# A factorization tower on one core: the last tile's softmax in two parts, its field jobs partly inside the loop

## The chip, the core and the metric

The kernel runs on one core of one Trainium2 chip. The metric is the device time of one execution in microseconds, less is better; a run of the kernel before took 1276.11 us in the median of three (1275.78 to 1276.74).

## The reference, cut to what matters

For each of 1024 samples, 33 rows of 128 numbers are gathered from 33 tables. All 528 pairs of them are multiplied element by element, go through a linear layer with relu, and are scored against a feature row of the sample. A softmax over the 528 scores weights the pair products, whose sum goes into a small perceptron.

```
inner = x[:, row] * x[:, col]                      # [1024, 528, 128]
fm = relu(einsum('bpd,ad->bpa', inner, attn_W) + attn_b)
scores = einsum('ba,bpa->bp', gnn_feature, fm)
attn = softmax(scores, axis=1)
attn_output = einsum('bp,bpd->bd', attn, inner) * 100.0
h = relu(concat([gnn_feature, attn_output, gnn_feature]) @ W_top1 + b_top1)
y = relu(h @ W_top2 + b_top2) @ W_top3
```

## The kernel before

The samples go in T = 8 tiles of 128, and a tile in STEPS = 32 steps of GROUPS = 4 samples; S counts the ALL = 256 steps of the program, s those within a tile t. The code is one block per engine, with semaphores between them, and the order of the work is written out by hand.

In step S, DVE multiplies the pairs of step S + 3 (`product`, L405) and forms the low part of step S + 1 (`rest_of_inner`, L412); ACT rounds the high part of S + 2 (`round_inner`, L298) and takes the hidden layer out of PSUM with bias and relu (`relu`, L290); PE runs `hidden(S)` (L534 for a native chunk, L541 to L543 for three passes of a split one). Per step 5 chunks, one of them native, two in the steps with s in NATIVE_2 = (2, 5, 8, 11, 14, 17); the remainder that ACT and DVE treat is then 1688 or 1696 columns, or 1264 or 1272. Behind every second step `reduce_steps` (L564) adds two steps' rows to `scores`: matmuls with a block matrix that put the scores of sample 32 j + s into row 32 j + s and add zeros elsewhere. PSUM has three banks for hidden chunks and all other jobs, in a ring in the order of `units`; `claim` waits until the bank's last user was taken out.

The softmax of tile t - 1 runs in the first steps of tile t: row maximum on DVE (L426, s = 1), exponentials on ACT (L305, s = 2), reciprocal of the sum on DVE (L430, s = 2), scaling on ACT into `attn` (L313, s = 3), and `turn_attn` on DVE (s = 4): the far half of the pairs is added (L436) and the matrix is transposed in blocks of 32 into `attn_turned` (L439). PE may begin the next tile's scores only behind the exponentials. SP then copies `attn_turned` in four pieces of partitions per job into the zero-filled `attn_t` (`spread_attn`, L207) and loads the rows of the fields from DRAM (`load_fields`, L202). Four `fields` jobs follow on PE (L592, at s = 7, 10, 13, 16), each for 32 samples, that is 8 steps; DVE multiplies each by x (`weigh`, L447) and sums it (`sum_weighted`, L454). Three `mlp` jobs end the tile.

The last tile has no next one. Behind step 255 come, in order: the softmax, ACT and DVE copying attn_turned into attn_t and into a part of `inner` that POOL has zeroed (L382, L386, L508, L512), all four jobs, with the fields of jobs 2 and 3 from `x_rows`, four products and sums, and the perceptron. PE fills pauses with `keep_clock` (L621): matmuls whose result nobody reads, 12, 8, 3 and 3 of them.

## Time and profile before

| | |
|---|---|
| median of 3 runs | 1276.11 us |
| the profiled execution: time | 1276.58 us |
| the profiled execution: span | 1274.3 us |
| PE busy | 1207.8 us, 95% |
| DVE busy | 1150.6 us, 90% |
| ACT busy | 1018.7 us, 80% |
| POOL busy | 465.7 us, 37% |

The span runs from the first to the last instruction of the profiled execution; its own time is 2.3 us longer. A row of a timeline gives the start in us from the span's start, the duration, the engine, the line, the operation, its tiles as out<-in, the shape, the number of merged instructions (x2) and, in brackets, the idle time before it and what ended it. PE's records of an fp32 matmul are two per instruction.

### The profile page before, as it was taken

How to read it: one execution, taken by the hardware profiler on the slowest of the kernel's cores; microseconds unless marked ns; L12 is line 12 of the kernel's file. 1: busy time of each engine (PE TensorE's matmuls, PEld its weight loads, DVE VectorE, ACT ScalarE, POOL GpSimd, SP SyncE). 2: the span in 40 equal slices, each digit the busy share in tenths (PEclk: the TensorE clock that was granted, in tenths of full speed). 3: DMA queues.
4: the chain of work that ended last, by engine and by line, in shares of the span. 5: the costliest groups of instructions: out<-in, count | busy, mean ns of one | idle time of the engine just before them, and what ended most of it. 6: DMA issues, size and time to landing. Idle time of an engine off the chain costs nothing.

```text
span 1274.3 us, 21264 instructions
## 1 busy us (share of the span) xinstructions
PE 1207.8 (95%) x8752; PEld 902.5 (71%) x8752; DVE 1150.6 (90%) x643; ACT 1018.7 (80%) x1038; POOL 465.7 (37%) x271
## 2 busy tenths in 40 slices
PE   1499999999999999999999999999999999999998
PEld 1277777777777777777767777677776777777776
DVE  2399899998999989998999989999899998999974
ACT  1288998778887888878897788877888788887882
POOL 6586684018810387006840088102880000000000
PEclk9999999999999999999999999999999999999999
DMA  4213211311103111131102211031111300012100
GB/s 107 101 34 96 55 30 28 110 36 30 30 18 126 30 27 32 30 106 36 32 21 58 93 30 32 18 110 41 30 32 31 107 17 1 1 30 57 31 1 1
DMA packets 54287, 58.47 MB, mean 46 GB/s; under 512 B 10536, under 2 KB 48560, under 8 KB 53168
## 3 DMA queue, kind: packets, MB, share of 16 engines
q1 hardware_dynamic: 45728, 39.81, 10.5%
q0 software_dynamic: 8448, 17.32, 5.2%
q8 instruction: 69, 1.13, 0.4%
q14 instruction: 26, 0.21, 0.1%
q10 hardware_dynamic: 16, 0.00, 0.0%
HBM read 36.12 MB, written 17.31 MB: 42 GB/s over the span
## 4 chain that ended last, share of the span: by engine, by line
PE 78%; ACT 7%; issue 7%; DVE 6%; POOL 2%; DMA 0%; DVEq 0%; ACTq 0%; POOLq 0%
PE scores L564 18%; PE ring L534 16%; PE ring L541 12%; PE ring L542 11%; PE ring L543 11%; PE ring L592 3%; ACT fm L290 3%; DVE inner L405 3%; POOL x_rows L259 2%; PE ring L574 2%; ACT inner_hi L298 2%; DVE inner_lo L412 2%; PE ring L610 1%; DVE attn L447 1%; PE scores L621 1%
## 5 line engine op out<-in xcount | busy, mean ns | idle before, releaser
L290 ACT ACTIVATE fm<-ring,attn_b_sb 128x848 f32<-128x848 f32 (+1 forms) x640 | 596.9, 971 | 182.1 <-PE ring L534 175.7
L405 DVE TENSOR_TENSOR inner<-xt 128x2112 f32<-128x2112 f32 x256 | 602.7, 2354 | 67.5 <-ACT xt L328 37.4
L259 POOL DMA_INDIRECT x_rows<-in_tbl,ids_all x264 | 463.2, 1754 | 490.9 <-PE ring L574 401.2
L412 DVE TENSOR_TENSOR inner_lo<-inner,inner_hi 128x1688 fp32r<-128x1688 f32 (+4 forms) x256 | 467.0, 1824 | 25.8 <-ACT inner_hi L298 22.8
L541 PE MATMUL ring<-inner_hi,attn_wt_lo 128*128 128x424 f32 (+1 forms) x971 | 434.8, 448 | 4.2 <-ACT fm L290 3.5
L298 ACT CAST inner_hi<-inner 128x1688 fp32r<-128x1688 f32 (+4 forms) x256 | 392.3, 1532 | 5.1 <-DVE inner L405 5.0
L542 PE MATMUL ring<-inner_lo,attn_wt_hi 128*128 128x424 f32 (+1 forms) x971 | 344.3, 355 | 0.0
L543 PE MATMUL ring<-inner_hi,attn_wt_hi 128*128 128x424 f32 (+1 forms) x971 | 344.1, 354 | 0.0
L534 PE MATMUL ring<-inner,attn_wt 128*128 128x424 f32 (+1 forms) x618 | 276.6, 544 | 10.2 <-issue 6.5
L564 PE MATMUL scores<-fm,gnn_blocks 128*32 128x264 f32 x4096 | 254.6, 389 | 5.5 <-ACT exp_pairs L305 5.5
L541 PEld LDWEIGHTS ring<-inner_hi,attn_wt_lo 128*128 128x128 f32 x971 | 182.8, 188 | 71.8 <-issue 39.1
L542 PEld LDWEIGHTS ring<-inner_lo,attn_wt_hi 128*128 128x128 f32 x971 | 183.3, 189 | 43.5 <-issue 40.3
L564 PEld LDWEIGHTS scores<-fm,gnn_blocks 128*32 128x32 f32 x4096 | 119.9, 109 | 107.2 <-issue 13.9
L543 PEld LDWEIGHTS ring<-inner_hi,attn_wt_hi 128*128 128x128 f32 x971 | 182.5, 188 | 5.5
L534 PEld LDWEIGHTS ring<-inner,attn_wt 128*128 128x128 f32 x618 | 104.8, 190 | 85.5 <-issue 76.9
L274 POOL MEMSET inner<- 128x2048 f32 x1 | 1.8, 1811 | 279.0 <-PE ring L543 279.0
L574 PE MATMUL ring<-ident,x_rows 128*128 128x128 f32 x264 | 39.2, 292 | 34.1 <-DMA x_rows<-in_tbl,ids_all 31.3
L328 ACT COPY xt<-ring 128x1024 f32<-128x1024 f32 (+1 forms) x40 | 38.5, 966 | 31.6 <-PE ring L574 20.8
L574 PEld LDWEIGHTS ring<-ident,x_rows 128*128 128x128 f32 x264 | 33.0, 151 | 39.6 <-DMA x_rows<-in_tbl,ids_all 25.2
L592 PE MATMUL ring<-attn_t,x_fields 128*128 128x128 f32 x480 | 58.3, 275 | 1.1 <-issue 1.1
L592 PEld LDWEIGHTS ring<-attn_t,x_fields 128*128 128x128 f32 x480 | 58.0, 191 | 1.7 <-issue 1.5
L447 DVE TENSOR_TENSOR attn<-ring,xt 128x1024 f32<-128x1024 f32 x32 | 39.0, 1219 | 3.2 <-PE ring L592 2.9
(50 smaller groups left out, 250.3 us busy)
## 6 DMA issues: line engine op xcount, KB each, us to landing
x_dram<-x_rows SPq DMA_DIRECT2D x8, 2112.0 KB, 6.6
x_fields<-x_dram SPq DMA_DIRECT2D x120, 128.0 KB, 3.0
x_rows<-in_tbl,ids_all POOLq DMA_INDIRECT x264
attn_t<-attn_turned SPq DMA_DIRECT2D x112, 32.0 KB, 1.9
w_sb<-in_W_top SPq DMA_DIRECT2D x2, 512.0 KB
x_rows<-x_dram SPq DMA_DIRECT2D x8, 128.0 KB, 3.9
x_fields<-in_r_gnn_feature SPq DMA_DIRECT2D x1, 512.0 KB
h<-in_W_top SPq DMA_DIRECT2D x1, 256.0 KB
```

What stands on the lines that cost most here:

```text
L259: nc.gpsimd.indirect_dma_start(out=x_rows[:, f, :], out_offset=None, in_=tables[f], in_offset=bass.IndirectOffsetOnAxis(ap=ids_all[:, t, f ...
L290: nc.scalar.activation(dst, slot(("hidden", pair, j))[:, :, 0:n], ACT.Relu, bias=attn_b_sb[:, 0:1]).then_inc(s_fm, 1)
L298: nc.scalar.copy(inner_hi[:, S % HI_BUFS, 0:COLS - at], inner[:, S % INNER_BUFS, at:]).then_inc(s_hi, 1)
L405: nc.vector.tensor_tensor(dst, a, b, ALU.mult).then_inc(s_inner, 1)
L412: nc.vector.tensor_tensor(inner_lo[:, S % LO_BUFS, 0:COLS - at], inner[:, S % INNER_BUFS, at:], inner_hi[:, S % HI_BUFS, 0:COLS - at].bitc ...
L534: nc.tensor.matmul(dst, attn_wt[:], inner[:, S % INNER_BUFS, begin:end], start=True, stop=True)\
L541: nc.tensor.matmul(dst, attn_wt_lo[:], hi, start=True, stop=False)
L542: nc.tensor.matmul(dst, attn_wt_hi[:], lo, start=False, stop=False)
L543: nc.tensor.matmul(dst, attn_wt_hi[:], hi, start=False, stop=True).then_inc(s_hidden, 1)
L564: last = nc.tensor.matmul(scores[I * j:I * j + I, h, 0:HALF], block_of(s, j), fm[:, S % FM_BUFS, at:at + HALF], start=s == 0, stop=s == ST ...
L574: last = nc.tensor.transpose(to[:, n // 4, n % 4 * P:(n % 4 + 1) * P], x_rows[:, FU * c + n, :], ident[:])
L592: last = nc.tensor.matmul(bank[:, h, to:to + QS * I], x[:, n, :], own[:, :, n, :], start=True, stop=True)
```

## The change

The table PART_END has nine parts in place of eight tiles: seven tiles, then 248 and 256. Part 7 is the first 24 steps (96 samples) of the last tile, and its softmax runs at steps 249 to 252. The scores stay in place and the last 8 steps are added; part 8 then repeats the softmax over all rows. Jobs 0 and 1 of the last tile stand behind `hidden(253)` and `hidden(254)`, with copies by SP; job 2 stands behind the last scores, from the same part 7. Only job 3 needs part 8. For it ACT scales the first 16 rows of the matrix and DVE the other 16, DVE transposes these first, then adds the far part and transposes the rest; the copies into attn_t are of 256 elements in place of twice 512. Job 3's products and sums go in halves of 16 samples, with job 2's sum between them. POOL's memset and the loads into x_rows are gone, and of the fillers 6 and 4 remain of 12 and 8.

```diff
+
+    PART_END = [STEPS * (t + 1) for t in range(T - 1)] + [ALL - FN, ALL]
+
+    def part_at(S, after):
+
+        return PART_END.index(S - after) if S - after in PART_END else None
+
+    LAST_FIELDS_AT = (ALL - 3, ALL - 2)
+
...
+        if S in LAST_FIELDS_AT:
+            jobs.append(("fields", T - 1, LAST_FIELDS_AT.index(S)))
         return jobs
...
-    units += [("fields", T - 1, c) for c in range(FJ)] + [("mlp", T - 1, n) for n in range(3)]
+    units += [("fields", T - 1, c) for c in (2, 3)] + [("mlp", T - 1, n) for n in range(3)]
...
-        TAIL_INNER = (ALL - 3) % INNER_BUFS
-        attn_t_tail = inner[:, TAIL_INNER, 0:2 * QS * FN * I].rearrange("p (c q n i) -> p c q n i", c=2, q=QS, n=FN)
-        x_fields_tail = x_rows[:, 0:2 * FN, :].rearrange("p (c n) d -> p c n d", c=2)
+        weighted_tail = inner[:, 0, 0:QS * FN * I].rearrange("p (b f) -> p b f", f=I)
...
-            sp.wait_ge(s_store, 16 * T)
-            sp.wait_ge(s_xt_done, XJ * T)
-            load_fields(T - 1, 2, x_fields_tail[:, 0], s_fields_tail)
-            load_fields(T - 1, 3, x_fields_tail[:, 1], s_fields_tail)
+            sp.wait_ge(s_inv, 3 * T)
+            spread_attn(0)
+            spread_attn(1)
+            sp.wait_ge(s_fields_done, FJ * (T - 1) + 1)
+            load_fields(T - 1, 2, x_fields[:, 0], s_fields[0])
+            spread_attn(2)
+            sp.wait_ge(s_fields_done, FJ * (T - 1) + 2)
+            load_fields(T - 1, 3, x_fields[:, 1], s_fields[1])
...
-            pool.wait_ge(s_lo, ALL - 2)
-            pool.wait_ge(s_hidden, CHUNKS * (ALL - 2))
-            nc.gpsimd.memset(inner[:, TAIL_INNER, 0:2 * QS * FN * I], 0.0).then_inc(s_tail_zero, 1)
...
+            def scale_attn(p):
+                act.wait_ge(s_inv, 3 * p + 1)
+                if p > 0:
+                    act.wait_ge(s_pooled, FJ * p if p < T else FJ * T - 2)
+                rows = I if p < T else K
+                src = exp_pairs[:].rearrange("b (i c) -> b i c", c=FX)[:, 0:rows, 1:F]
+                nc.scalar.activation(attn[:, 0:rows, :], src, ACT.Copy, scale=inv_sum[:, 0:1]).then_inc(s_attn, 1)
...
-                if s == EXP_AT and t > 0:
-                    exps(t - 1)
+                if part_at(S, EXP_AT) is not None:
+                    exps(part_at(S, EXP_AT))
                 if S + 2 < ALL:
                     round_inner(S + 2)
-                if s == SCALE_AT and t > 0:
-                    scale_attn(t - 1)
+                if part_at(S, SCALE_AT) is not None:
+                    scale_attn(part_at(S, SCALE_AT))
...
-            exps(T - 1)
-            scale_attn(T - 1)
-            act.wait_ge(s_inv, 3 * T)
-            act.wait_ge(s_fields_done, FJ * (T - 1))
-            act.wait_ge(s_tail_zero, 1)
+            exps(T)
+            scale_attn(T)
+            act.wait_ge(s_tail_high, 2)
+            act.wait_ge(s_inv, 3 * (T + 1))
+            act.wait_ge(s_fields_done, FJ * T - 2)
             for q in range(QS // 2):
                 own = slice(q * I, (q + 1) * I)
-                nc.scalar.copy(attn_t[own, :, q], attn_turned[own, 0:2 * FN, :].rearrange("p (c n) i -> p c n i", c=2))\
-                    .then_inc(s_tail_attn, 1)
-            for q in range(QS // 2):
-                own = slice(q * I, (q + 1) * I)
-                nc.scalar.copy(attn_t_tail[own, :, q], attn_turned[own, 2 * FN:, :].rearrange("p (c n) i -> p c n i", c=2))\
-                    .then_inc(s_tail_attn, 1)
+                nc.scalar.copy(attn_t[own, (FJ - 1) % 2, q], attn_turned[own, (FJ - 1) * FN:, :]).then_inc(s_tail_attn, 1)
...
+            def row_max(p):
+                dve.wait_ge(s_red, PART_END[p] // 2)
...
+            def add_far(p):
+                dve.wait_ge(s_attn, p + 1)
...
-                dve.wait_ge(s_inv, 3 * t + 2)
+                dve.wait_ge(s_inv, 3 * p + 2)
+
+            def turn_attn(p):
+                add_far(p)
                 nc.vector.transpose(attn_turned[:].rearrange("p n i -> p i n"), attn[:]).then_inc(s_inv, 1)
+
+            def turn_last_attn():
+                turned = attn_turned[:].rearrange("p n i -> p i n")
+                src = exp_pairs[:].rearrange("b (i c) -> b i c", c=FX)[:, K:I, 1:F]
+                dve.wait_ge(s_inv, 3 * T + 1)
+                nc.vector.tensor_scalar(attn[:, K:I, :], src, inv_sum[:, 0:1], None, ALU.mult).then_inc(s_tail_high, 1)
+                dve.wait_ge(s_tail_high, 1)
+                dve.wait_ge(s_spread[0], 16 * QS * (FJ // 2 * (T - 1) + 2))
+                nc.vector.transpose(turned[:, K:I, :], attn[:, K:I, :]).then_inc(s_tail_high, 1)
+                add_far(T)
+                nc.vector.transpose(turned[:, 0:K, :], attn[:, 0:K, :]).then_inc(s_inv, 1)
...
-                nc.vector.tensor_tensor(weighted, y, xt[:, t % 2, own, 0:I], ALU.mult).then_inc(s_weighted, 1)
+                dst = weighted if (t, c) != (T - 1, 2) else weighted_tail
+                nc.vector.tensor_tensor(dst, y, xt[:, t % 2, own, 0:I], ALU.mult).then_inc(s_weighted, 1)
...
+            def last_weighted_sum():
+                first, half = P - QS * FN, QS * FN // 2
+                y = slot(("fields", T - 1, FJ - 1))
+                for h in range(2):
+                    own = slice(first + h * half, first + (h + 1) * half)
+                    part = weighted[:, h * half:(h + 1) * half, :]
+                    if h == 0:
+                        dve.wait_ge(s_half, 1)
+                    else:
+                        dve.wait_ge(s_fields_done, FJ * T)
+                    nc.vector.tensor_tensor(part, y[:, h, :].rearrange("d (b f) -> d b f", f=I), xt[:, (T - 1) % 2, own, 0:I],
+                                            ALU.mult).then_inc(s_half_weighted if h == 0 else s_weighted, 1)
+                    if h == 0:
+                        dve.wait_ge(s_half_weighted, 1)
+                    else:
+                        dve.wait_ge(s_weighted, FJ * T)
+                    nc.vector.tensor_reduce(pooled[:, own], part, AX.X, ALU.add)\
+                        .then_inc(s_half_pooled if h == 0 else s_pooled, 1)
+                    if h == 0:
+                        sum_weighted(T - 1, 2)
+                dve.wait_ge(s_half_pooled, 1)
+                dve.wait_ge(s_pooled, FJ * T)
+                nc.vector.tensor_scalar(pooled[:], pooled[:], 100.0, None, ALU.mult).then_inc(s_pooled100, 1)
...
-                if s == TURN_AT and t > 0:
-                    turn_attn(t - 1)
+                if part_at(S, TURN_AT) is not None:
+                    turn_attn(part_at(S, TURN_AT))
...
+                if part_at(S, MAX_AT) is not None:
+                    row_max(part_at(S, MAX_AT))
                 if s == MAX_AT and t > 0:
-                    row_max(t - 1)
                     gnn_block(t)
-                if s == INV_AT and t > 0:
-                    invert_sum(t - 1)
-            row_max(T - 1)
-            invert_sum(T - 1)
-            turn_attn(T - 1)
-            dve.wait_ge(s_inv, 3 * T)
-            dve.wait_ge(s_fields_done, FJ * (T - 1))
-            dve.wait_ge(s_tail_zero, 1)
+                if part_at(S, INV_AT) is not None:
+                    invert_sum(part_at(S, INV_AT))
+            row_max(T)
+            invert_sum(T)
+            turn_last_attn()
+            dve.wait_ge(s_inv, 3 * (T + 1))
+            dve.wait_ge(s_tail_high, 2)
+            dve.wait_ge(s_fields_done, FJ * T - 2)
             for q in range(QS // 2, QS):
...
+                nc.vector.tensor_copy(attn_t[own, (FJ - 1) % 2, q], attn_turned[own, (FJ - 1) * FN:, :]).then_inc(s_tail_attn, 1)
+            weigh(T - 1, 2)
+            last_weighted_sum()
...
+                if S0 in PART_END:
+                    pe.wait_ge(s_exp, PART_END.index(S0) + 1)
                 if s0 == 0:
-                    if t > 0:
-                        pe.wait_ge(s_exp, t)
                     pe.wait_ge(s_blocks, t + 1)
...
-                if t < T - 1:
+                pe.wait_ge(s_fields[c % 2], 16 * QS * (FJ // 2 * t + c // 2 + 1))
+                if (t, c) != (T - 1, FJ - 1):
                     pe.wait_ge(s_spread[c % 2], 16 * QS * (FJ // 2 * t + c // 2 + 1))
-                    pe.wait_ge(s_fields[c % 2], 16 * QS * (FJ // 2 * t + c // 2 + 1))
-                elif c < 2:
-                    pe.wait_ge(s_tail_attn, 2 * QS)
-                    pe.wait_ge(s_fields[c], 16 * QS * (FJ // 2 * t + 1))
                 else:
-                    own, x = attn_t_tail[:, c % 2], x_fields_tail[:, c % 2]
-                    pe.wait_ge(s_fields_tail, 2 * 16 * QS)
+                    pe.wait_ge(s_tail_attn, QS)
                 for n in range(FN):
                     h, to = divmod(n * QS * I, 512)
                     last = nc.tensor.matmul(bank[:, h, to:to + QS * I], x[:, n, :], own[:, :, n, :], start=True, stop=True)
+                    if (t, c) == (T - 1, FJ - 1) and n == FN // 2 - 1:
+                        last.then_inc(s_half, 1)
...
-            pe.wait_ge(s_exp, T)
-            keep_clock(12)
-            for c in range(FJ):
-                fields(T - 1, c)
-            keep_clock(8)
+            fields(T - 1, 2)
+            pe.wait_ge(s_exp, T + 1)
+            keep_clock(6)
+            fields(T - 1, 3)
+            keep_clock(4)
```

DVE's last steps, before: from the remainder of step 250 on (inner_lo is the remainder, inner the product).

```order
L412 TENSOR_TENSOR inner_lo<-inner,inner_hi 128x1688
L405 TENSOR_TENSOR inner<-xt 128x2112
L412 TENSOR_TENSOR inner_lo<-inner,inner_hi 128x1696
L405 TENSOR_TENSOR inner<-xt 128x2112
L412 TENSOR_TENSOR inner_lo<-inner,inner_hi 128x1688
L405 TENSOR_TENSOR inner<-xt 128x2112
L412 TENSOR_TENSOR inner_lo<-inner,inner_hi 128x1696
L405 TENSOR_TENSOR inner<-xt 128x2112
L412 TENSOR_TENSOR inner_lo<-inner,inner_hi 128x1688
L412 TENSOR_TENSOR inner_lo<-inner,inner_hi 128x1696
```

And now, from the product of step 252 on:

```order
L413 TENSOR_TENSOR inner<-xt 128x2112
L434 TENSOR_REDUCE neg_max<-scores 128x1
L420 TENSOR_TENSOR inner_lo<-inner,inner_hi 128x1696
L413 TENSOR_TENSOR inner<-xt 128x2112
L438 RECIPROCAL inv_sum<-exp_sum 128x1
L420 TENSOR_TENSOR inner_lo<-inner,inner_hi 128x1688
L413 TENSOR_TENSOR inner<-xt 128x2112
L420 TENSOR_TENSOR inner_lo<-inner,inner_hi 128x1696
L444 SCALAR_TENSOR_TENSOR attn<-exp_pairs,inv_sum,attn 128x16x16
L450 STREAM_TRANSPOSE attn_turned<-attn 128x32x32
L413 TENSOR_TENSOR inner<-xt 128x2112
L420 TENSOR_TENSOR inner_lo<-inner,inner_hi 128x1688
```

Maximum, reciprocal, far part (L444) and transposition (L450) stand between the products and remainders of steps 251 to 255.

PE behind the last scores, before:

```order
L564 MATMUL scores<-fm,gnn_blocks 32x264 x16
L621 MATMUL scores<-fm,attn_wt 128x264 x12
L592 MATMUL ring<-attn_t,x_fields 128x128 x16
L592 MATMUL ring<-inner,x_rows 128x128 x16
L621 MATMUL scores<-fm,attn_wt 128x264 x8
L600 MATMUL ring<-gnn_t,w_sb 128x128 x4
L604 MATMUL ring<-pooled,w_sb 128x128 x4
```

And now:

```order
L607 MATMUL scores<-fm,gnn_blocks 32x264 x16
L631 MATMUL ring<-attn_t,x_fields 128x128 x8
L662 MATMUL scores<-fm,attn_wt 128x264 x6
L631 MATMUL ring<-attn_t,x_fields 128x128 x8
L662 MATMUL scores<-fm,attn_wt 128x264 x4
L641 MATMUL ring<-gnn_t,w_sb 128x128 x4
L645 MATMUL ring<-pooled,w_sb 128x128 x4
L662 MATMUL scores<-fm,attn_wt 128x264 x3
```

One job stands ahead of the first filler and one behind it. The two others stand in the loop; the first of them behind the last three-pass chunk of step 253 and ahead of the native chunk of step 254:

```order
L584 MATMUL ring<-inner_hi,attn_wt_lo 128x424
L585 MATMUL ring<-inner_lo,attn_wt_hi 128x424
L586 MATMUL ring<-inner_hi,attn_wt_hi 128x424
L631 MATMUL ring<-attn_t,x_fields 128x128 x8
L577 MATMUL ring<-inner,attn_wt 128x424
L584 MATMUL ring<-inner_hi,attn_wt_lo 128x424
```

## Rows read from the trace of the kernel before

**Rows 1.** The page, part 1: busy us (share of the span) of each engine, and instructions.

```profile
PE 1207.8 (95%) x8752; PEld 902.5 (71%) x8752; DVE 1150.6 (90%) x643; ACT 1018.7 (80%) x1038; POOL 465.7 (37%) x271
```

**Rows 2.** Timeline of PE behind the loop: start us, us, engine, line, op, tiles, count.

```profile
1246.76 5.61 PE L621 MATMUL scores<-fm,attn_wt 128*128 128x264 f32 x24 [2.09 <-ACT exp_pairs L305]
1253.49 3.81 PE L592 MATMUL ring<-attn_t,x_fields 128*128 128x128 f32 x32 [1.12 <-issue]
```

**Rows 3.** Timeline of DVE behind the loop.

```profile
1244.74 0.71 DVE L426 TENSOR_REDUCE neg_max<-scores 128x1 f32<-128x528 f32 x1 [8.33 <-PE scores L564]
1246.74 0.16 DVE L430 RECIPROCAL inv_sum<-exp_sum 128x1 f32<-128x1 f32 x1 [1.30 <-ACT exp_pairs L305]
1248.15 0.67 DVE L436 SCALAR_TENSOR_TENSOR attn<-exp_pairs,inv_sum,attn 128x256 f32<-128x256 f32 x1 [1.24 <-ACT attn L313]
1248.85 1.96 DVE L439 STREAM_TRANSPOSE attn_turned<-attn 128x1024 f32<-128x1024 f32 x1
1250.85 0.87 DVE L508 COPY attn_t<-attn_turned 32x512 f32<-32x512 f32 x2
...
1255.55 1.22 DVE L447 TENSOR_TENSOR attn<-ring,xt 128x1024 f32<-128x1024 f32 x1 [2.92 <-PE ring L592]
1256.81 1.22 DVE L454 TENSOR_REDUCE pooled<-attn 128x32 f32<-128x1024 f32 x1
...
1265.81 0.23 DVE L457 TENSOR_SCALAR pooled<-pooled 128x128 f32<-128x128 f32 x1
```

**Rows 4.** Timeline of ACT behind the loop.

```profile
1246.94 1.18 ACT L313 ACTIVATE attn<-exp_pairs,inv_sum 128x1024 f32<-128x1024 f32 x1 [0.23 <-DVE inv_sum L430]
1250.85 1.26 ACT L382 COPY attn_t<-attn_turned 32x512 f32<-32x512 f32 x2 [2.73 <-DVE attn_turned L439]
```

**Rows 5.** Timeline of PE, steps 224 to 232: matmuls of one pair of steps onto scores.

```profile
1099.62 1.99 PE L564 MATMUL scores<-fm,gnn_blocks 128*32 128x264 f32 x32
...
1108.75 1.99 PE L564 MATMUL scores<-fm,gnn_blocks 128*32 128x264 f32 x32 [0.77 <-ACT exp_pairs L305]
...
1117.69 1.99 PE L564 MATMUL scores<-fm,gnn_blocks 128*32 128x264 f32 x32
...
1125.97 1.99 PE L564 MATMUL scores<-fm,gnn_blocks 128*32 128x264 f32 x32
```

**Rows 6.** The same, steps 230 and 231.

```profile
1136.29 1.99 PE L564 MATMUL scores<-fm,gnn_blocks 128*32 128x264 f32 x32
```

**Rows 7.** The same, steps 248 to 251.

```profile
1220.86 1.99 PE L564 MATMUL scores<-fm,gnn_blocks 128*32 128x264 f32 x32
...
1229.08 1.99 PE L564 MATMUL scores<-fm,gnn_blocks 128*32 128x264 f32 x32
```

**Rows 8.** Timeline of DVE, step 228: the turn of tile 6.

```profile
1116.39 2.11 DVE L439 STREAM_TRANSPOSE attn_turned<-attn 128x1024 f32<-128x1024 f32 x1
```

**Rows 9.** The page, part 5: busy, mean ns of one | idle before, releaser.

```profile
L405 DVE TENSOR_TENSOR inner<-xt 128x2112 f32<-128x2112 f32 x256 | 602.7, 2354 | 67.5 <-ACT xt L328 37.4
...
L412 DVE TENSOR_TENSOR inner_lo<-inner,inner_hi 128x1688 fp32r<-128x1688 f32 (+4 forms) x256 | 467.0, 1824 | 25.8 <-ACT inner_hi L298 22.8
```

**Rows 10.** Timeline of ACT, steps 227 and 229: rounding of 1272 and 1696 columns.

```profile
1112.53 1.25 ACT L298 CAST inner_hi<-inner 128x1272 fp32r<-128x1272 f32 x1
...
1121.46 1.60 ACT L298 CAST inner_hi<-inner 128x1696 fp32r<-128x1696 f32 x1
```

**Rows 11.** Timeline of PE, step 228: a wait for ACT.

```profile
1115.77 0.46 PE L541 MATMUL ring<-inner_hi,attn_wt_lo 128*128 128x424 f32 x1 [0.51 <-ACT fm L290]
```

**Rows 12.** Timeline of the SP queue, step 228: the eight copies of attn_turned.

```profile
1118.53 4.94 SPq L207 DMA_DIRECT2D attn_t<-attn_turned  x8
```

**Rows 13.** DMA by tile, attn_t: time from issue to landing over all 112.

```profile
DMA to landing us min/median/max: 1.8/1.9/3.6
```

**Rows 14.** Busy time by engine (PE, PEld, DVE, ACT, POOL), PEclk, DMA share, GB/s.

```profile
1266.10:1274.30 8.20, 6.36 (x40) 5.04 (x40) 0.00 (x0) 2.02 (x7) 0.00 (x0) 1.00 0.00 1
```

**Rows 15.** Timeline of PE, first step of the program.

```profile
54.64 5.99 PE L534 MATMUL ring<-inner,attn_wt 128*128 128x424 f32 x8 [6.46 <-issue]
```

More of the change, by code:

```diff
@@ L306, in exps @@
                                      bias=neg_max[:, 0:1], accum_out=exp_sum[:, 0:1]).then_inc(s_exp, 1)
-            def scale_attn(t):
-                act.wait_ge(s_inv, 3 * t + 1)
-                if t > 0:
-                    act.wait_ge(s_pooled, FJ * t)
-                src = exp_pairs[:].rearrange("b (i c) -> b i c", c=FX)[:, 0:I, 1:F]
-                nc.scalar.activation(attn[:], src, ACT.Copy, scale=inv_sum[:, 0:1]).then_inc(s_attn, 1)
+            def scale_attn(p):
[5 more added lines that the diff above has]
+                nc.scalar.activation(attn[:, 0:rows, :], src, ACT.Copy, scale=inv_sum[:, 0:1]).then_inc(s_attn, 1)
             def repeat(t, c):
@@ L453, in sum_weighted @@
                     dve.wait_ge(s_mlp_done, 3 * (t - 1) + 1)
-                nc.vector.tensor_reduce(pooled[:, own], weighted, AX.X, ALU.add).then_inc(s_pooled, 1)
+                src = weighted if (t, c) != (T - 1, 2) else weighted_tail
+                nc.vector.tensor_reduce(pooled[:, own], src, AX.X, ALU.add).then_inc(s_pooled, 1)
                 if c == FJ - 1:
@@ L645, in _ @@
             reduce_steps(ALL - 2, True)
-            pe.wait_ge(s_exp, T)
-            keep_clock(12)
-            for c in range(FJ):
-                fields(T - 1, c)
-            keep_clock(8)
+            fields(T - 1, 2)
[3 more added lines that the diff above has]
+            keep_clock(4)
             for n in range(3):
```

27 lines of the change are left out of this document (8 added, 19 removed).

## The prediction

> **What bounds the kernel now.** First read the page's busy shares: PE is busy for 95% of the span and DVE for 90% [rows 1], so inside the loop an added matmul is paid in full, and added DVE or ACT work only as far as PE comes to wait for it. Then read the timelines behind the loop. There the order is another: from 1244.74, when DVE begins the last maximum, the work is one chain through the softmax, the turn, the copies into attn_t, four products and four sums on DVE, and the scaling of pooled, which ends at 1265.81 + 0.23 = 1266.04 [rows 3]. That chain is 21.30 us. The perceptron and the store behind it take another 8.2 us, 6.36 of them PE's [rows 14]. PE works in the 21.30 us too, but half of it is filler (5.61 us [rows 2]). So the change trades the time of a nearly idle tail against the time of a full loop, and the question is the rate of exchange. I call M the start of the last maximum, and count the tail from it.
>
> **Part 1: the second softmax inside the loop.** Part 7 (96 samples) runs its maximum, exponentials, scaling and turn at steps 249 to 252, placed as at a tile's border. The trace has this event seven times, so I price it from the last one, at steps 225 to 228. Between two plain pairs of score matmuls lie 1229.08 - 1220.86 = 8.22 us [rows 7]. At the border the same distances are 1108.75 - 1099.62 = 9.13, 1117.69 - 1108.75 = 8.94 and 1125.97 - 1117.69 = 8.28 [rows 5]: 0.91 + 0.72 + 0.06 over plain. The first surplus is PE's wait for the exponentials (0.77). The second holds a wait of 0.51 for a relu of ACT [rows 11], which ACT reaches late behind the scaling of attn. The third pair has a step with two native chunks, which the new place hasn't, so I drop the 0.06. Sum: 1.63 us. The new place is a little worse. At step 227 ACT rounds only 1272 columns (1.25 us), at step 251 it rounds a full remainder (1.60 us) [rows 10], ahead of the scaling and of the relu that PE waits for. I add the whole 0.35: **+1.98 us**. Ends: 1.63 (the ACT queue absorbs it) and 2.6 (the surplus is paid again in the next pair).
>
> **Part 2: jobs 0 and 1 of the last tile in the loop.** Two jobs behind the loop took 3.81 us [rows 2], so 1.90 each; inside the loop a pair with one job lasts 1136.29 - 1125.97 = 10.32 against 8.28, so 2.04 [rows 5, 6]. Nothing hides them, PE has no idle time there. I take 2 x 1.90 = **+3.80 us**, ends 3.6 and 4.1.
>
> **Part 3: do their operands come in time?** In the other tiles three steps lie between the turn and job 0, here one. At step 228 the transposition ends at 1116.39 + 2.11 = 1118.50 [rows 8]. SP issues the eight copies from 1118.53 in 4.94 us, 0.62 each, and one lands 1.9 us after its issue in the median [rows 12, 13]. Job 0 needs four: the fourth is issued at 1118.53 + 3 x 0.62 = 1120.4 and lands at 1122.3. PE would want it one score group and one step behind 1117.69: a plain pair is two steps and 1.99 of scores, so 1117.69 + 1.99 + (8.22 - 1.99) / 2 = 1122.8. Margin 0.5 us, and the later relu shifts PE by 0.35 more, while DVE's turn is some 0.2 later (a full remainder in place of a short one, no gnn blocks). So I cost it at nothing, and its upper end is 1.2: a landing of 3.6 us, the longest seen, less the 1.9 and the margin. Job 1 needs the eighth, issued at 1118.53 + 7 x 0.62 = 1122.9 and landed at 1124.8, and PE asks for them two us of job and three of matmuls later. Job 2's loads and copies (8 issues) start when job 0 is done, some 12 us ahead of the loop's end; job 3's loads start when job 1 is done. Both lie under steps 254 and 255.
>
> **Part 4: DVE's extra work in the loop.** Maximum, reciprocal, far half and transposition are 0.71 + 0.16 + 0.67 + 1.96 = 3.5 us [rows 3], and two products and sums follow. The cover is DVE's lead. Behind the transposition it owes one product (2.35) and the remainder for step 254 (1.9 at most [rows 9]: a full one is slower than the mean of 1.82), so it is done near 1118.5 + 4.3 = 1122.8 by the clock of step 228. PE needs that remainder behind job 0 and the first chunk of step 254, near 1125. From there DVE has no products left, only PE has. Cost nothing. Without that cover PE would wait the overshoot, and I keep 0.5 as the end. The POOL memset, the eight loads into x_rows and the filler go at no gain: nothing waited for them.
>
> Loop: 1.98 + 3.80 = **+5.8 us**, between 5.2 and 7.5.
>
> **Part 5: the new tail.** Maximum, exponentials and reciprocal are as before, ending at M + 2.16 (1246.74 + 0.16 [rows 3]). Job 2 on PE hides in the 2.09 us in which PE only waited for the exponentials [rows 2]. Then, on DVE:
> - scaling the upper 16 rows, 512 elements. No row shows it; a copy of 512 is 0.42 (0.87 for two), a reduction of 528 is 0.71 [rows 3]. It reads and writes SBUF as the copy does: 0.42, done M + 2.62. ACT scales the lower rows beside it, half of 1.18 and half its fixed share, 0.7 [rows 4], done M + 2.9, covered.
> - transposing half: 1.96 / 2 plus a few hundredths, 1.02; far part 0.67; the other half 1.02, with 0.03 between: M + 5.42. Before: 1250.81, M + 6.07.
> - copies of 256 elements, two on ACT and two on DVE. ACT took 1.26 for two of 512 [rows 4], 0.62 each. Its roundings give 0.35 us for 424 elements [rows 10], 0.83 ns per element, so 256 elements less are 0.21 less: 0.43 with gaps each, M + 6.31. Before there were four of 512 and PE began at 1253.49, M + 8.75; now M + 6.41.
> - DVE's own copies end near M + 6.02, then the product of job 2, 1.22, to M + 7.29. Half of job 3 is ready at M + 6.41 + 1.1 = 7.51 (a whole one took 1255.55 - 1253.49 = 2.06). Product of a half 0.71 (as the 528 of the maximum), sum of it 0.71, sum of job 2 1.22, product and sum of the second half 0.71 + 0.71, scaling 0.23, and 0.24 of gaps: 7.52 + 4.29 + 0.24 = M + 12.05.
>
> Before M + 21.30, now M + 12.05: **-9.3 us**. Ends: -9.8 (halves at exactly half) and -8.5 (the scaling 0.71, each half transposition 1.2, copies still 0.6). PE's part from there to the store is the same.
>
> A rule bears on the halves. By the row the ACT copy of 512 is 0.617, and the slope leaves 0.20 of it fixed. The Trainium skill, page "VectorE: DVE Perf Modes", section "The TRN2 errata — SBUF-src ops pay a fixed extra latency per instruction", says that splitting pays a fixed latency per piece, and gives ScalarE 224 cycles plus the elements. By its figures (an estimate) a copy of 256 is 0.40 us where I have 0.43, and the tail would be 0.06 shorter; for 512 the trace agrees, 0.61 to 0.62.
>
> **Sum.** +5.8 - 9.3 = -3.5 us. The profiled execution took 1276.58 (span 1274.3), 0.5 over the median of 1276.11. Against the median I forecast **1272.6 us**. A change within 0.2%, 2.55 us, is no change for a measurement of this kernel.
>
> **Rivals.**
> - *The turn comes too close to job 0.* The fourth copy lands late (1.2), or DVE's lead is short (0.5), or the border costs 2.6; the loop then pays 6.8 to 7.5 and 1.8 to 2.5 us are left: near 1274.0. For it: a margin of 0.5 us against a landing that varies by 1.8 [rows 13], and full remainders where the border has short ones. Against it: PE is delayed by the same ACT work. Chance 0.17.
> - *The clock falls in the tail (slower).* Twenty filler matmuls ahead of the perceptron become ten, and PE idles from M + 4.9 to M + 6.4. The granted clock is 1.00 (2.4 GHz) in the tail now [rows 14], behind idle stretches of 2.09 and 1.12 us [rows 2]. At the start, behind 6.46 us of idle, eight matmul records of 424 columns took 5.99 us, 0.75 each [rows 15]; the filler has 0.23 for 264 columns [rows 2], which is 0.38 for 424, so those ran at half pace. If the granted clock fell to 1.2 GHz at the last gap, 1.1 us of job 3 and the 6.36 us of PE behind the sum would double: +7.5 - 3.5 = +4.0, 1280.1 us. It decides if the clock is already down when job 3 begins. Against it: no new gap is longer than 2.09 us. The Trainium skill, page "TensorE: Matmul & The Clock Gate", section "What's actually happening", has throttled as the default state and activity as what releases it, which speaks against less filler; by it the time would be those 1280.1 us. Chance 0.05.
> - *The tail gains more.* Halves cost half, the ACT delay is absorbed: 5.3 - 9.8 = -4.5, 1271.6 us. Chance 0.10.
>
> **The numbers.** The forecast has 0.66, the rest 0.02. The range takes the ends of loop and tail, 1271.4 to 1274.7; outside are the clock and a border dearer than all seven seen. Faster by over 0.2% means below 1273.56: forecast, the better tail and a little of the first rival, 0.78. Same: most of that rival, 0.16. Slower: 0.06.
>
> **What would show it.** Last score matmul some 5.8 us later than at 1244.7; distances of about 9.1, 9.3 and 12.0 between the score groups of 246 to 252; PE waiting under 0.3 us ahead of job 0; from the maximum to the scaled pooled 12.0 us; PEclk 1.00 to the end. Wrong would be a wait for DMA ahead of job 0, a wait of PE for inner_lo at step 254, or matmul records of 0.75 us behind job 3.

## The result, and the profile after

| | before | changed |
|---|---|---|
| median | 1276.11 us (8 runs, 1275.73 to 1276.74) | 1272.16 us (8 runs, 1272.02 to 1272.48) |
| profiled execution, time | 1276.58 us | 1272.05 us |
| span | 1274.3 us | 1269.9 us |

The ratio is 0.9968, with a 95% interval of 0.9959 to 0.9977: 3.95 us faster. On the page the busy times hardly moved. PE has 4.3 us and 20 records less, which are the ten fillers; DVE has 2.7 us more [rows 1].

```profile
PE 1203.5 (95%) x8732; PEld 898.6 (71%) x8732; DVE 1153.3 (91%) x649; ACT 1018.9 (80%) x1039; POOL 465.4 (37%) x270
```

The timeline of PE at steps 246 to 255, with the score groups and the two jobs that now stand in the loop (start, duration, engine, line, form, in brackets the wait before it):

```profile
1212.27 1.99 PE L607 MATMUL scores<-fm,gnn_blocks 128*32 128x264 f32 x32
...
1221.40 1.99 PE L607 MATMUL scores<-fm,gnn_blocks 128*32 128x264 f32 x32 [0.85 <-ACT exp_pairs L317]
...
1228.77 0.46 PE L584 MATMUL ring<-inner_hi,attn_wt_lo 128*128 128x424 f32 x1 [0.87 <-ACT fm L302]
...
1230.70 1.99 PE L607 MATMUL scores<-fm,gnn_blocks 128*32 128x264 f32 x32
...
1235.74 1.95 PE L631 MATMUL ring<-attn_t,x_fields 128*128 128x128 f32 x16
...
1240.55 1.95 PE L631 MATMUL ring<-attn_t,x_fields 128*128 128x128 f32 x16
1242.42 1.99 PE L607 MATMUL scores<-fm,gnn_blocks 128*32 128x264 f32 x32
...
1247.70 2.23 PE L607 MATMUL scores<-fm,gnn_blocks 128*32 128x264 f32 x32
```

The distances between the groups are 1221.40 - 1212.27 = 9.13, 9.30, 11.72 and 5.28 us. In the kernel before they are 8.22, three times (one of them in [rows 7]), and 5.14. From the group of step 246 to DVE's last maximum it is 1249.99 - 1212.27 = 37.72 us, before 32.10 (from 1212.64 to 1244.74 [rows 3]). The loop is **5.62 us longer**: 0.91 and 1.08 us at the new border, 3.50 in the distance that holds both jobs, and 0.14 in the last. The two waits of PE in it are those that the border of a tile has: 0.85 for the exponentials, 0.87 for a relu of ACT [rows 5, 11: 0.77 and 0.51]. Ahead of job 0 at 1235.74 PE waits for nothing.

The timeline of DVE behind the loop, which answers to [rows 3]:

```profile
1249.99 0.71 DVE L434 TENSOR_REDUCE neg_max<-scores 128x1 f32<-128x528 f32 x1 [4.98 <-PE scores L607]
...
1252.19 0.48 DVE L456 TENSOR_SCALAR attn<-exp_pairs,inv_sum 128x512 f32<-128x512 f32 x1
1252.71 1.08 DVE L459 STREAM_TRANSPOSE attn_turned<-attn 128x512 f32<-128x512 f32 x1
1253.65 0.58 DVE L444 SCALAR_TENSOR_TENSOR attn<-exp_pairs,inv_sum,attn 128x256 f32<-128x256 f32 x1
1254.26 1.05 DVE L461 STREAM_TRANSPOSE attn_turned<-attn 128x512 f32<-128x512 f32 x1
1255.35 0.61 DVE L557 COPY attn_t<-attn_turned 32x256 f32<-32x256 f32 x2
1255.99 1.23 DVE L470 TENSOR_TENSOR inner<-ring,xt 128x1024 f32<-128x1024 f32 x1
1257.54 0.69 DVE L493 TENSOR_TENSOR attn<-ring,xt 128x512 f32<-128x512 f32 x1 [0.33 <-PE ring L631]
1258.27 0.69 DVE L499 TENSOR_REDUCE pooled<-attn 128x16 f32<-128x512 f32 x1
1258.87 1.21 DVE L478 TENSOR_REDUCE pooled<-inner 128x32 f32<-128x1024 f32 x1
1259.99 0.68 DVE L493 TENSOR_TENSOR attn<-ring,xt 128x512 f32<-128x512 f32 x1
...
1261.50 0.23 DVE L505 TENSOR_SCALAR pooled<-pooled 128x128 f32<-128x128 f32 x1
```

From the start of the maximum to the end of the scaling of pooled it is 1261.73 - 1249.99 = **11.74 us, before 21.30**. The transposed matrix is complete at +5.32 (before +6.07), and two products and two sums of a whole job are gone.

ACT's scaling of half a matrix and its two copies [rows 4], and PE around them [rows 2]:

```profile
1252.19 0.74 ACT L326 ACTIVATE attn<-exp_pairs,inv_sum 128x512 f32<-128x512 f32 x1 [0.23 <-DVE inv_sum L438]
1255.39 0.83 ACT L395 COPY attn_t<-attn_turned 32x256 f32<-32x256 f32 x2 [2.46 <-DVE attn_turned L461]
```

```profile
1249.85 2.05 PE L631 MATMUL ring<-attn_t,x_fields 128*128 128x128 f32 x16
...
1256.37 2.02 PE L631 MATMUL ring<-attn_t,x_fields 128*128 128x128 f32 x16 [1.42 <-ACT attn_t L395]
```

Job 2 runs while DVE and ACT are at the maximum and the exponentials. Behind the scaled pooled both kernels take 8.22 us to the end of the span. So +5.62 - 9.56 = -3.94 us by the two traces, against -3.95 by the medians. The remaining 0.4 us between the two spans lies ahead of step 222, in code that the change doesn't touch: its scores start at 1099.62 before and at 1099.26 after.

### The profile page after: what moved, and what is told of

The parts are those of the page before. It is cut to its first block, busy times and chain, and to the rows that moved or that the text cites. A ratio compares the mean times of both kernels' runs of the same rounds, so it can differ in the third digit from the quotient of the medians.

```text
span 1269.9 us, 21243 instructions
## 1 busy us (share of the span) xinstructions
PE 1203.5 (95%) x8732; PEld 898.6 (71%) x8732; DVE 1153.3 (91%) x649; ACT 1018.9 (80%) x1039; POOL 465.4 (37%) x270
## 4 chain that ended last, share of the span: by engine, by line
PE 77%; ACT 8%; issue 7%; DVE 6%; POOL 2%; DMA 0%; DVEq 0%; ACTq 0%; POOLq 0%
PE scores L607 18%; PE ring L577 16%; PE ring L584 12%; PE ring L585 11%; PE ring L586 11%; ACT fm L302 3%; PE ring L631 3%; DVE inner L413 3%; ACT inner_hi L310 3%; POOL x_rows L274 2%; PE ring L617 2%; DVE inner_lo L420 2%; PE ring L651 1%; ACT exp_pairs L317 1%; DVE attn L470 1%
## 5 line engine op out<-in xcount | busy, mean ns | idle before, releaser
L631 PE MATMUL ring<-attn_t,x_fields 128*128 128x128 f32 x512 | 62.5, 275 | 1.4 <-ACT attn_t L395 1.4
L631 PEld LDWEIGHTS ring<-attn_t,x_fields 128*128 128x128 f32 x512 | 61.9, 191 | 2.4 <-issue 2.2
L478 DVE TENSOR_REDUCE pooled<-attn 128x32 f32<-128x1024 f32 x30 | 36.4, 1214 | 0.1
```

The lines of the kernel that those rows point to most:

```text
L631: last = nc.tensor.matmul(bank[:, h, to:to + QS * I], x[:, n, :], own[:, :, n, :], start=True, stop=True)
```

## The experiments

Runs 1 to 4 were made on chip 11 and runs 5 to 12 on chip 0, where the kernel before takes 1273.28 us (beside runs 1 to 4), 1273.94 (5 to 8) and 1273.18 (9 to 12). Most of the difference from 1276.11 lies ahead of the first scores (67.5 us into the span of the changed kernel above, 64.8 in run 12), so distances inside a trace are compared. All runs but 10 and 12 are single executions. For the changed kernel these are, above and within 0.01 us in run 12 too, 37.72 us from the scores of step 246 to the last maximum (the loop's end), 11.74 us from there to the scaled pooled (the tail), and 8.22 us to the end. The edits of runs 1, 2 and 4 don't touch the loop, and it takes 37.71 to 37.72 us in them; those of runs 5 to 8 don't touch the tail, and it takes 11.74 to 11.75. So a difference of 0.1 us between two such distances is clear of noise. M + x is x us behind the start of the last maximum.

**1. Job 3 in one piece.** Is the order of job 3's halves and job 2's sum worth something?

```diff
-            weigh(T - 1, 2)
-            last_weighted_sum()
+            for c in (2, 3):
+                weigh(T - 1, c)
+                sum_weighted(T - 1, c)
```

> Job 3's product and sum in one piece, behind job 2's sum; the turn stays in halves. Theory 1 (DVE bounds the last stage, and job 2 covers PE's part): job 3 is ready 8.4 us behind the start of the last maximum (6.4 + 2.0), and DVE reaches it at 8.5 anyway (copies done at 6.0, product 1.23, sum 1.21). So the halves start nothing earlier and only pay the fixed share of two more instructions: scaled pooled at 11.3 us in place of 11.74, the run 0.4 us shorter. Theory 2 (the halves let DVE begin half a job earlier): 12.3 to 12.5, 0.6 us longer.

Measured: loop 37.72, tail **11.32**, 0.42 less. DVE's timeline, with M at 1247.13:

```profile
1254.39 1.22 DVE L478 TENSOR_REDUCE pooled<-inner 128x32 f32<-128x1024 f32 x1
1255.71 1.23 DVE L470 TENSOR_TENSOR attn<-ring,xt 128x1024 f32<-128x1024 f32 x1
1256.97 1.22 DVE L478 TENSOR_REDUCE pooled<-attn 128x32 f32<-128x1024 f32 x1
1258.23 0.23 DVE L481 TENSOR_SCALAR pooled<-pooled 128x128 f32<-128x128 f32 x1
```

Job 3 is complete on PE at M + 8.41, and DVE takes it at M + 8.58, directly behind job 2's sum. Halves can't end the chain earlier, because job 2's product and sum fill the time. They cost the fixed share of two more instructions (twice 0.69 for the halves against 1.23 for a whole product, and much the same for the sum, 0.3 us in all). In the order of the changed kernel DVE also waits 0.33 us for the first half of job 3 (at 1257.54 above) while job 2's sum stands ready; run 1 has no such wait. The overlaps between instructions take a part of the two back. Theory 1 holds. This part of the change loses time.

**2. The turn in one piece.** ACT scales all 32 rows, one transposition; job 3 stays in halves.

```diff
-                rows = I if p < T else K
+                rows = I
...
-            turn_last_attn()
+            dve.wait_ge(s_spread[0], 16 * QS * (FJ // 2 * (T - 1) + 2))
+            turn_attn(T)
...
```

> Scaling on ACT of all 32 rows and one transposition, as before the change; job 3's products stay in halves. Theory 1 (the split puts DVE's scaling and first transposition beside ACT's scaling): the transposition ends 6.07 us behind the start of the maximum in place of 5.32, and all behind it moves by 0.75: the run 0.75 us longer. Theory 2 (the fixed share of the added instructions eats it): below 0.3 us longer.

Measured: tail 12.46, **0.72 more**. With M at 1246.96:

```profile
1250.44 0.66 DVE L443 SCALAR_TENSOR_TENSOR attn<-exp_pairs,inv_sum,attn 128x256 f32<-128x256 f32 x1 [1.31 <-ACT attn L326]
1251.13 1.92 DVE L449 STREAM_TRANSPOSE attn_turned<-attn 128x1024 f32<-128x1024 f32 x1
```

DVE waits 1.31 us for ACT's scaling, which the split fills with its own half, and the transposition ends at M + 6.09 in place of 5.32. Theory 1 holds: of the two things that the change does in halves, this one pays.

**3. Job 1 behind the scores.** Only job 0 stays in the loop, and job 1's product goes into another buffer.

```diff
-    LAST_FIELDS_AT = (ALL - 3, ALL - 2)
+    LAST_FIELDS_AT = (ALL - 3,)
...
+            fields(T - 1, 1)
             fields(T - 1, 2)
...
+            weigh(T - 1, 1)
+            sum_weighted(T - 1, 1)
             weigh(T - 1, 2)
             last_weighted_sum()
```

> Job 1 behind the scores too, so that only job 0 stands in the loop; DVE's product and sum of job 1 come ahead of those of job 2. Theory 1 (a job costs the loop 1.87 us of PE and spares the tail 2.5 us of DVE): loop 1.9 us shorter, tail 2.5 us longer, the run 0.6 us longer. Theory 2 (the tail has idle DVE time and takes the job for nothing): 1.9 us shorter.

Measured: loop 35.83 (-1.89), tail 13.94 (+2.20), and 9.43 us behind it in place of 8.22, which neither theory had. The perceptron's first product with pooled on PE, and two stretches of the windows view (the stretch and its length, busy us of PE, PEld, DVE, ACT and POOL, then PEclk, DMA share and GB/s):

```profile
1259.04 2.08 PE L648 MATMUL ring<-pooled,w_sb 128*128 128x128 f32 x8 [2.88 <-DVE pooled L506]
```

```profile
1256.00:1259.00 3.00, 0.16 (x2) 0.00 (x0) 2.85 (x5) 0.00 (x0) 0.00 (x0) 0.94 0.00 0
1259.00:1261.00 2.00, 1.96 (x9) 1.96 (x10) 0.00 (x0) 0.00 (x0) 0.00 (x0) 0.50 0.00 0
```

PE waited 2.88 us for the longer tail, the granted clock fell to half (1.2 GHz) before the wait was over, and eight records took 2.08 us in place of 1.16. So this run didn't price the job alone. Run 11 repeats it with nine fillers in place of four.

```diff
-            keep_clock(4)
+            keep_clock(9)
```

> Job 1 behind the scores as before, with nine filler matmuls in place of four ahead of the perceptron. Theory 1 (the perceptron ran slow there because the clock fell in a PE pause of 2.9 us, and the job's own balance is 1.93 us less in the loop and 2.2 more in the tail): granted clock 1.00 to the end, 8.2 us from the scaled pooled to the end in place of 9.43, and 0.3 us longer than the changed kernel from the first scores to the end. Theory 2 (something else slows the perceptron): 9.4 us stay.

```profile
1256.00:1260.00 4.00, 3.34 (x24) 2.96 (x23) 2.72 (x5) 0.00 (x0) 0.00 (x0) 1.00 0.00 0
1260.00:1267.10 7.10, 5.28 (x33) 3.96 (x31) 0.00 (x0) 2.02 (x7) 0.00 (x0) 1.00 0.00 0
```

Measured: clock 1.00, 8.21 us behind the tail, loop 35.81, tail 13.93: -1.91 + 2.19 = **+0.28 us** on the changed kernel. A job in the loop costs 1.9 us there and spares the tail 2.2. That is the rate of exchange, and it is thin: the times of single executions don't resolve it (1269.14 us here, 1269.12 to 1269.74 for the changed kernel in run 12).

**4. No filler.** The other question of the clock: do the ten fillers that are left hold it?

```diff
-            keep_clock(6)
             fields(T - 1, 3)
-            keep_clock(4)
```

> The ten filler matmuls ahead of the perceptron left out (they compute nothing that is read). PE then idles from 2.0 to 6.4 us behind the start of the maximum. Theory 1 (this idle time is short enough for the clock to stay at 2.4 GHz): granted clock 1.00 to the end, job 3 at 2.0 us, the run as long as the changed kernel within 0.2 us. Theory 2 (filler is what holds the clock): granted clock below 1 behind job 3 or in the perceptron, the records there of up to twice the length, and the run up to 7.5 us longer.

```profile
1253.20 3.26 PE L631 MATMUL ring<-attn_t,x_fields 128*128 128x128 f32 x16 [4.42 <-ACT attn_t L395]
```

```profile
1249.00:1253.00 4.00, 0.00 (x0) 0.00 (x0) 3.80 (x8) 1.49 (x3) 0.00 (x0) 1.00 0.00 0
1253.00:1254.30 1.30, 1.10 (x7) 1.13 (x8) 1.04 (x1) 0.05 (x1) 0.00 (x0) 0.78 0.01 6
1254.30:1256.50 2.20, 2.20 (x13) 2.20 (x12) 1.67 (x3) 0.00 (x0) 0.00 (x0) 0.50 0.00 0
```

Measured: through the 4.42 us of idle PE the granted clock is still 1.00. It falls when job 3 has begun (0.78 in the mean of 1253.0 to 1254.3, 0.50 behind it), job 3 takes 3.26 us in place of 2.02, and the tail 12.12, **0.38 more**. From 1258 on the clock is 1.00 again and the perceptron takes its usual 8.21. Theory 2 is right that the clock falls without the fillers, and the price is far below its upper end: DVE's work on job 2 covers most of a slow job 3 (DVE waits 0.75 us for its first half in place of 0.33), and the clock is back before the perceptron. The Trainium skill, page "TensorE: Matmul & The Clock Gate", section "What's actually happening", calls the throttled state the default that activity lifts; the traces agree in both runs: 0.50 behind pauses of 2.88 and 4.42 us, and 1.00 again while PE works.

**5. Jobs 0 and 1 one step earlier.** How near are the copies of attn_turned to job 0?

```diff
-    LAST_FIELDS_AT = (ALL - 3, ALL - 2)
+    LAST_FIELDS_AT = (ALL - 4, ALL - 3)
```

> Jobs 0 and 1 one step earlier, behind steps 252 and 253. Theory 1 (part 3 of the prediction: the fourth copy of attn_turned lands just ahead of job 0, 0.45 us in the changed kernel, and one place earlier PE would wait for it): PE asks for it at the place where the scores of step 250 began, 1230.7, the copy lands at 1235.3, a wait of 4.6 us, and the loop is 4 to 4.7 us longer. Theory 2 (there is slack behind the turn that the forecast did not count): below 1 us longer.

```profile
1232.54 3.75 PE L631 MATMUL ring<-attn_t,x_fields 128*128 128x128 f32 x16 [4.58 <-DMA attn_t<-attn_turned]
```

```profile
1235.00:1240.00 5.00, 5.00 (x42) 2.84 (x41) 2.44 (x2) 0.00 (x0) 0.00 (x0) 0.68 0.36 104
```

Measured: PE waits **4.58 us** for the DMA, as theory 1 has it. The loop is 45.18 us though, 7.46 more: in that pause the clock fell too. It is 0.50 from 1232 to 1238 (0.68 in the mean of 1235 to 1240), job 0 took 3.75 us, and what follows it is slow until the clock has risen. Six us at half the clock are 3 us lost, by estimate, and 7.46 - 4.58 = 2.88 were. No theory had that. In the changed kernel SP issues the eight copies here:

```profile
1231.63 4.94 SPq L218 DMA_DIRECT2D attn_t<-attn_turned  x8
```

The fourth is issued at 1231.63 + 3 x 0.62 = 1233.5 and lands 1.9 later [rows 13], at 1235.4; PE takes job 0 at 1235.74.

**6. The exponentials ahead of the relu.** Three relus stand on ACT between the maximum and the exponentials. This moves the exponentials up by one relu, at all eight borders inside the loop.

```diff
-                relu(S // 2, 2 if S % 2 else 0)
                 if part_at(S, EXP_AT) is not None:
                     exps(part_at(S, EXP_AT))
+                relu(S // 2, 2 if S % 2 else 0)
```

> On ACT the exponentials stand ahead of the first relu of their step in place of behind it, at all eight borders inside the loop. Theory 1 (PE's wait of 0.77 to 0.85 us at a border is ACT's queue: the maximum is there 1.9 us before the exponentials begin, and three relus stand between): first distance at a border 8.3 in place of 9.14, the loop 6 us shorter over eight borders. Theory 2 (ACT is full there, and the relu that now comes later makes PE wait as long): each border keeps its sum of 18.07 us within 0.2, the loop within 1 us.

Measured: the first distance at a border is 8.32 in place of 9.14 (1096.52 to the first row below), as theory 1 has it, and the second 9.00 in place of 8.93. But nothing is won: the fourth distance, with job 0 of the tile before, grows from 10.31 to 11.08. Summed over the four it is 36.66 us with the old order (run 5, whose tile borders are those of the changed kernel) and 36.70 now. From the first scores to those of step 246, with all seven borders of tiles, it is 1145.10 us here, and 1145.01 and 1145.13 in runs 5 and 12. PE's timeline:

```profile
1104.84 1.99 PE L607 MATMUL scores<-fm,gnn_blocks 128*32 128x264 f32 x32
...
1132.45 0.46 PE L584 MATMUL ring<-inner_hi,attn_wt_lo 128*128 128x416 f32 x1 [0.72 <-DVE attn L470]
...
1232.82 2.02 PE L631 MATMUL ring<-attn_t,x_fields 128*128 128x128 f32 x16 [0.36 <-DMA attn_t<-attn_turned]
```

The wait is now at 1132.45, for `weigh` on DVE (0.72 us). Both theories were about ACT, and both fall. The windows view of the four distances, in the changed kernel and in this run:

```profile
1099.26:1135.92 36.66, 35.38 (x254) 25.56 (x253) 36.26 (x24) 31.37 (x32) 0.00 (x0) 1.00 0.09 22
1096.52:1133.22 36.70, 35.40 (x254) 25.56 (x253) 36.25 (x24) 32.09 (x33) 0.00 (x0) 1.00 0.10 24
```

DVE is busy for 36.26 of 36.66 us and for 36.25 of 36.70, PE for 35.4. So a tile's border is as long as DVE's queue makes it; which engine PE waits for depends on where it comes first.

The last tile's border is another case. Its loop is 37.54, 0.18 shorter, and what takes the rest back is a wait of 0.36 us for the copies of attn_turned ahead of job 0 (1232.82). The maximum and the transposition behind it are as far apart as before (14.04 us from the start of the one to the end of the other, 14.08 in the changed kernel), so with PE 0.8 us earlier the copies come too late.

**7. A native chunk more at step 253.** ACT and DVE then treat 1272 columns of it in place of 1696.

```diff
+    NATIVE[ALL - 3] = 2
```

> Step 253 with two native chunks, so that ACT and DVE treat 1272 of its columns and not 1696. Theory 1 (the 0.35 us by which the new border is dearer is ACT's longer rounding ahead of the scaling): PE's wait for the relu 0.5 us in place of 0.87, the distance from the scores of 248 to those of 250 8.94 in place of 9.30; the native chunk costs PE 0.13 in the next one; the loop 0.2 us shorter. Theory 2 (the 0.35 has another cause): the distance stays at 9.3.

```profile
1218.54 1.99 PE L608 MATMUL scores<-fm,gnn_blocks 128*32 128x264 f32 x32 [0.84 <-ACT exp_pairs L318]
...
1225.54 0.46 PE L585 MATMUL ring<-inner_hi,attn_wt_lo 128*128 128x424 f32 x1 [0.51 <-ACT fm L303]
...
1227.47 1.99 PE L608 MATMUL scores<-fm,gnn_blocks 128*32 128x264 f32 x32
```

Measured: the wait for the relu is 0.51, the distance 1227.47 - 1218.54 = 8.93 in place of 9.30, the next 11.89 in place of 11.72 (0.17 for the native chunk, 0.13 expected); the loop is 37.52, 0.20 less. Theory 1 holds.

**8. The scaling one relu later,** at the seven borders of tiles, on top of run 6.

```diff
-                if part_at(S, SCALE_AT) is not None:
-                    scale_attn(part_at(S, SCALE_AT))
+                scaled = part_at(S, SCALE_AT)
+                if scaled == T - 1:
+                    scale_attn(scaled)
                 relu(S // 2, 3 if S % 2 else 1)
+                if scaled is not None and scaled < T - 1:
+                    scale_attn(scaled)
```

> As with the exponentials ahead of the relu, and at the seven borders of tiles the scaling of attn one relu later. Theory 1 (PE's second wait at a border, 0.51 us, is for a relu behind the scaling): the second distance 8.3 to 8.4 in place of 8.93, 3.5 to 4.5 us less over seven borders than with the exponentials moved alone. Theory 2 (the scaling then holds up DVE's turn and the products behind it): the third distance grows by as much, no gain.

```profile
1112.58 0.45 PE L587 MATMUL ring<-inner_hi,attn_wt_lo 128*128 128x416 f32 x1 [0.27 <-ACT fm L302]
...
1132.20 0.46 PE L587 MATMUL ring<-inner_hi,attn_wt_lo 128*128 128x416 f32 x1 [0.79 <-DVE attn L473]
...
1233.06 2.02 PE L634 MATMUL ring<-attn_t,x_fields 128*128 128x128 f32 x16 [0.85 <-DMA attn_t<-attn_turned]
```

Measured: the four distances are 8.32, 8.70, 8.49 and 11.14. The second shrank, with a wait for ACT of 0.27 in place of 0.58 in run 6. The third and fourth gave it back, the fourth with a wait for DVE of 0.79: 36.65 us in sum, DVE busy for 36.20 of them, the same sum as with the old order. Theory 2 holds, and the reading of run 6 stands: waits move, the sum doesn't.

The last tile's order is that of run 6, but job 0 waits 0.85 us for the copies in place of 0.36, and the loop is 38.04, 0.32 above the changed kernel. SP took 5.52 us to issue the eight copies here and 5.03 in run 6, 4.94 in the changed kernel. Why the issue times differ was not tried; they show how thin the margin ahead of job 0 is.

**9. Jobs 0 and 1 one step later,** on top of run 6; job 1's product stands behind the loop and its sum behind the maximum.

```diff
-    LAST_FIELDS_AT = (ALL - 3, ALL - 2)
+    LAST_FIELDS_AT = (ALL - 2, ALL - 1)
...
+            weigh(T - 1, 1)
             row_max(T)
+            sum_weighted(T - 1, 1)
             invert_sum(T)
```

> The exponentials ahead of the relu, and jobs 0 and 1 of the last tile one step later, behind steps 254 and 255; job 1's product stands behind the loop, its sum in DVE's wait for the exponentials. Theory 1 (with the exponentials first, what takes the gain back at the last border is job 0 waiting for DVE's product and for the copies of its operand): both waits go, 37.0 to 37.3 us from the scores of step 246 to the last maximum, in place of 37.72 in the changed kernel and 37.55 with the exponentials first alone. Theory 2 (DVE's own queue bounds the last steps too): 37.5 or more.

```profile
1217.77 1.99 PE L609 MATMUL scores<-fm,gnn_blocks 128*32 128x264 f32 x32
...
1227.12 1.99 PE L609 MATMUL scores<-fm,gnn_blocks 128*32 128x264 f32 x32
...
1237.24 1.99 PE L609 MATMUL scores<-fm,gnn_blocks 128*32 128x264 f32 x32
...
1244.31 1.99 PE L609 MATMUL scores<-fm,gnn_blocks 128*32 128x264 f32 x32
```

```profile
1246.37 0.71 DVE L434 TENSOR_REDUCE neg_max<-scores 128x1 f32<-128x528 f32 x1 [0.72 <-PE scores L609]
1246.99 1.21 DVE L478 TENSOR_REDUCE pooled<-attn 128x32 f32<-128x1024 f32 x1
```

Measured: distances 8.33, 9.35, 10.12 and 7.07, and the loop is **36.93**, 0.79 below the changed kernel. Job 0 now waits for nothing. The maximum starts 2.06 us behind the start of the last score group, before 2.29, where PE took 2.23 us for a group that takes 1.99 elsewhere; job 1 ahead of it gives ACT the time for the last relus. That the pause was one for these relus is read from the order of the work. The sum of job 1 fits into DVE's wait for the exponentials. Theory 1 holds in kind, with 0.07 us more gained than it gave. The two distances of the border give 0.75 of the 0.79 us (8.33 + 9.35 against 9.13 + 9.30). So at the last tile's border the exponentials ahead of the relu are worth 0.75 us, once job 0 stands where it doesn't wait for the copies. The later jobs with the old order on ACT were not run.

**10 and 12. The parts together, and the changed kernel again.** The edits of runs 1, 6, 7 and 9 in one kernel, five executions, beside the changed kernel, six.

> The parts that helped together: exponentials ahead of the relu, jobs 0 and 1 one step later, two native chunks at step 253, job 3's product and sum in one piece. By the parts alone: 0.5 to 0.7 us in the loop, 0.2 from the native chunk, 0.4 in the tail: 1.0 to 1.3 us below the changed kernel on the same chip. If the parts hide each other, 0.4.

> The changed kernel itself, on the chip and in the rounds of the combined version, as its measure: 0.9968 of the kernel before within 0.0005, and the same distances between its own score groups as in its first profile.

| | median, us | ratio to the kernel before | 95% interval | loop | tail |
|---|---|---|---|---|---|
| changed kernel again | 1269.20 (1269.12 to 1269.74) | 0.9968 | 0.9956 to 0.9981 | 37.73 | 11.74 |
| the parts together | 1267.60 (1267.28 to 1267.71) | 0.9955 | 0.9941 to 0.9969 | 36.53 | 11.32 |

The combined kernel is 1.60 us faster than the changed one by the medians, whose runs don't overlap, and 1.20 + 0.42 = 1.62 by the traces. Both forecasts of that gain were lower. The native chunk was worth 0.40 there (36.93 to 36.53) and not 0.20: it shortens the distance behind the border to 8.99 as in run 7, but the next one, 10.09, doesn't grow in return (10.12 in run 9). By the timelines the native chunk costs PE its 0.16 us there too (step 253 takes 3.28 us, in run 9 3.12), but step 254 takes 3.02 in place of 3.21. In run 9 PE loses some 0.1 us at each of two matmuls of it (0.46 us long in place of 0.36); in run 10 DVE begins its last two remainders 0.46 us earlier (1230.42 for 1230.88), and both losses are gone. Whether DVE is their cause was not tried by itself.

## Why the prediction was right

The forecast was 1272.6 us, the result is 1272.16. Loop and tail both came out a little better than forecast (+5.62 for +5.8, -9.56 for -9.3), so no two errors hid each other. The bounds don't quite follow from the ends of the parts: 5.2 - 9.8 gives 1271.5 us and 7.5 - 8.5 gives 1275.1, where the text has 1271.4 and 1274.7; the result lies inside either. By its steps:

- **Part 1, the border in the loop: +1.98 forecast, 0.91 + 1.08 = 1.99 measured.** Pricing it from the seventh border, plus the 0.35 us of longer rounding, was right to 0.02, and run 7 shows that the 0.35 is that rounding. The explanation was only half right: it named two waits for ACT as the surplus. Runs 6 and 8 show that at a tile's border DVE's queue keeps the sum whatever ACT does. At the new border ACT's order does cost, 0.75 us by runs 6 and 9. That the number held is explained by the new border's repeating the order of the old one on all engines; this was not tested by itself.
- **Part 2, two jobs: +3.80 forecast, 3.50 + 0.14 = 3.64 measured.** In the loop the next matmul starts 1.78 us behind job 0 (1235.74 to 1237.52) and 1.87 behind job 1 (1240.55 to 1242.42), where the 1.90 of the tail's row contains the end of its last matmul; the low end of 3.6 was nearly right.
- **Part 3, operands in time: margin 0.5 us forecast.** By the rows 0.3 to 0.4, and no wait. One step earlier the wait is 4.58 us, and with PE 0.8 us earlier it is 0.36 (run 6) or 0.85 (run 8). The step was right, and it is the thinnest of the five.
- **Part 4, DVE's work covered: right.** The remainder for step 254 is done at 1233.70 + 1.90 = 1235.60, and PE takes that step's first split chunk at 1237.91, 2.3 us later; the text has 2.2 (1125 less 1122.8). With PE 0.8 us earlier it is the copies that PE meets in the last tile, and DVE only at the borders of tiles. In run 9, where job 0 stands behind that step, PE loses 0.2 us in it; job 0 may have been a part of the cover.
- **Part 5, the tail: 12.05 forecast, 11.74 measured.** The turn ends at +5.32 for 5.42: DVE's half scaling 0.48 (0.42 forecast), the far part 0.58 (0.67), and an instruction that waits for no result of the one before starts 0.09 to 0.14 us ahead of its end (the far part at 1253.65, with the transposition busy until 1253.79). The copies are as forecast (0.83 for two; 0.86). Job 3 starts at +6.38 (6.41). The rest are two such overlaps around job 2's sum, where I had counted gaps. What the step lacked is the comparison with whole pieces: it took the halves of job 3 as given, and they cost 0.42.
- **The rivals.** The turn too close to job 0 did not happen, though it was near. The clock did not fall in the changed kernel; its mechanism is real, by runs 3, 4 and 5, but its price was far off: 0.38 us for a pause of 4.4 us ahead of job 3, and 1.2 us where the pause stood directly ahead of the perceptron, and not 7.5. The 7.5 took the clock as low from job 3 to the end, and in both runs it was back at 1.00 within 4 us. The better tail of the last rival (M + 11.5 by its -9.8) came half of the way.
